# Two-layer mixture-of-experts kernel: both waves' lists cleared by whole stores, first list rows in buffers of their own, list tables and first mixing product moved at the border

## The chip, the cores and the metric

One core of a Trainium2 chip. The metric is the time of one execution on the device in microseconds, the median of three runs. The engines are TensorE (PE), VectorE (DVE), ScalarE (ACT), GpSimd (POOL) and SyncE (SP, which here only issues DMAs).

## The reference

x is 64 samples x 64 channels x 1024 positions in float32. Two layers, each with a residual:

```
x = x + L0_ffn(L0_cond(x, cond_128, ...))
x = x + L1_ffn(L1_cond(x, cond_128, ...))
L0_cond: grouped 1-d convolution (4 groups, 9 taps) + cond @ c_weight.T + bias
L0_ffn:  y @ base_w.T + base_b + 0.5 * sum over the top 2 of 16 experts of w_e * (y @ A.T) @ B_e.T
L1_cond: a 2-layer MLP gives 8 attention weights per sample; out = (sum_k att_k W_k) x + att @ bias_k
L1_ffn:  y @ base_W.T + sum over the top 2 of 28 experts of 2 * g_e * (y @ lora_A_e.T) @ lora_B_e.T
```

## The kernel before, in words

**Tiles.** Rows are (sample, channel) pairs; a tile is 128 rows (2 samples) x 1024 columns, so there are 32 tiles. Every float32 product is made of three float32r products: high x high, high x low, low x high (`three`, L1349 to L1353). So each operand is split in two parts: ACT copies the high one (L736), DVE subtracts for the low one.

**Layer 0, `step0` per tile.** PE convolves tile t+2 (`conv`, into banks c0 and c1), turns tile t+1 (`turn_conv`) and multiplies tile t's y with the weights in three column blocks (`over_y`): bank z2 first (256 base columns, 64 columns of A, 16 router columns), then z0, then z1 (384 columns each), 24 matmuls per block. DVE routes from z2 (`routing`, `list0`), adds the residuals (`residual`, L1199), makes the low parts (`x8_low`, `y_low` L979) and computes each row's rank in its expert's list (`rank0`; the operation at L1036 that writes `before` is the one PE's next block z2 waits for). POOL adds the bias to the next x (L651).

**Lists.** The expert products of layer 0 are not done per tile but over lists sorted by expert, in two waves of 16 tiles. `list0` writes the tile's 64 values times both gate weights into `listed` (L1026), `rank0` the places into `place`, and POOL scatters both rows sets by indirect DMA into `hs_dram[w]` (`scatter`, L665). There is one `listed` buffer of 2 x 64 values; before it is written again, all scatters so far must have landed (semaphore `listed_out`). Behind each expert's list up to the end of a tile of 128 the rows have to be zero. For wave 1 the whole of `hs_dram[1]` is cleared by 17 stores of 512 KB from a zeroed `zt[3]` in steps 12 to 15 (`clear_lists`, L436). For wave 0 16 stores of 128 x 64 zeros go behind the ends of the lists once the counts are known, in step 16 (`pad_lists`, L431 and L432).

**Tables.** When a wave's 16 tiles are ranked, PE and DVE make the tables in three rounds: `count_lists` (rows per expert, tiles per expert), `first_tiles` with DVE's `tiles_of_lists` (prefix sum), `list_tables` (expert and row tile of each of the 48 listed tiles; DVE copies them at L1179 and L1180). `listed_places` (L1187 to L1193) finds every row's place in the results. Then SP reads the tables by register (`value_load`, L442 and L446) and issues four `ht` loads (L443) and four `bd` loads (L449) per listed step (`start_lists`, `listed_step`); PE turns them (`turn_ht`, L1405) and multiplies (`listed_pair`). Wave 0's listed steps run beside tiles 18 to 29, wave 1's beside layer 1's tiles 2 to 13.

**Layer 1, `step1` per tile.** POOL gathers and adds each row's two results from `zs_dram` onto x1 (L677, L685). DVE and ACT build the sample's mixing matrix (`mix`: L1121 to L1130), PE multiplies it with x1 (`mixing`), turns the result (`turn_mixed`, L1474) and runs it over the weights in z2 (252 columns), z0 and z1 (512 each) and over the lora product (`over_h`). The transposes of `hx` (L1601) wait for DVE's routing (`spread1`).

**The border.** Tile 31 of layer 0 and tile 0 of layer 1 overlap. The weights of layer 1 lie where those of layer 0 lay, so each block is split once layer 0's last products on it are done (`w1_high` on ACT, `w1_low` on DVE, L1071; the profile names them `w_0l` and `w_1l`). `mixing(0)` stands between block z0 and block z1 of tile 31. The order on every engine is the order of the program; only semaphores tie engines together.

**SP's order in a step of layer 0:** load `x8raw` of tile t+2 (L407; it waits for the convolution before it), store x1 of tile t-1 (L419), then lists or pads, then load x of tile t+3 (L401; it waits for POOL's residual).

## Time and profile before

| | |
|---|---|
| median of three runs | 1268.43 us (1264.81 to 1268.62) |
| profiled execution, its own time | 1271.76 us |
| its span | 1269.6 us |
| mean granted clock of PE | 0.993 |
| busy: PE, DVE, ACT, POOL | 97%, 50%, 30%, 22% |
| DMA | 258.59 MB, 204 GB/s in the mean |

The time of the profiled execution includes some 2 us around the span. "PE waits" are idle times of PE before an instruction, with what ended them; "DMA to landing" is the time from the issue to the last byte. Names such as `x8raw<-in_x_dram` are output<-input; "PEclk" or "granted clock" is the share of TensorE's 2.4 GHz that it was given.

### The profile page before, as it was taken

How to read it: one execution, taken by the hardware profiler on the slowest of the kernel's cores; microseconds unless marked ns; L12 is line 12 of the kernel's file. 1: busy time of each engine (PE TensorE's matmuls, PEld its weight loads, DVE VectorE, ACT ScalarE, POOL GpSimd, SP SyncE). 2: the span in 40 equal slices, each digit the busy share in tenths (PEclk: the TensorE clock that was granted, in tenths of full speed). 3: DMA queues.
4: the chain of work that ended last, by engine and by line, in shares of the span. 5: the costliest groups of instructions: out<-in, count | busy, mean ns of one | idle time of the engine just before them, and what ended most of it. 6: DMA issues, size and time to landing. Idle time of an engine off the chain costs nothing.

```text
span 1269.6 us, 22120 instructions
## 1 busy us (share of the span) xinstructions
PE 1237.0 (97%) x7264; PEld 1095.3 (86%) x7264; DVE 633.1 (50%) x1809; ACT 376.5 (30%) x801; POOL 279.9 (22%) x309
## 2 busy tenths in 40 slices
PE   6999999999899999998989999999999999999998
PEld 6999999999899999997778787887888888888887
DVE  6666666576444445455645334243344354354452
ACT  4312222121243343324233333334412222222221
POOL 2222222332222222243311121112121211211200
PEclk9999999999899999998999999999999999999999
DMA  7346666665989999967699999999865455455410
GB/s 281 122 141 197 204 192 236 243 233 156 285 272 307 292 306 317 296 226 215 119 227 288 269 269 281 243 299 291 251 145 116 88 120 111 96 118 107 103 50 33
DMA packets 85040, 258.59 MB, mean 204 GB/s; under 512 B 25489, under 2 KB 29969, under 8 KB 77714
## 3 DMA queue, kind: packets, MB, share of 16 engines
q1 hardware_dynamic: 72464, 221.73, 54.3%
q0 software_dynamic: 11264, 35.66, 16.2%
q10 hardware_dynamic: 1266, 0.70, 0.2%
q8 instruction: 15, 0.25, 0.1%
q14 instruction: 31, 0.25, 0.1%
HBM read 154.24 MB, written 103.81 MB: 203 GB/s over the span
## 4 chain that ended last, share of the span: by engine, by line
PE 50%; DVE 2%; DMA 2%; issue 1%; SPq 0%; ACT 0%; POOL 0%; ACTq 0%; POOLq 0%
PE z L1351 14%; PE z L1353 14%; PE z L1352 14%; PE t L1474 2%; PE c L1351 1%; DMA xin<-zs_dram,gpos 1%; PE c L1353 1%; PE c L1352 1%; PE c L1416 1%; PE c L1418 1%; PE prep L1601 1%; PE c L1420 1%; DMA ht<-hs_dram 0%; DVE w_1l L1071 0%; PE t L1420 0%
## 5 line engine op out<-in xcount | busy, mean ns | idle before, releaser
L1351 PE MATMUL z<-w_1h,yh 128*128 128x512 f32 (+1 forms) x504 | 189.0, 375 | 0.0
L1351 PE MATMUL z<-w_0h,yh 128*128 128x512 f32 (+1 forms) x504 | 187.4, 372 | 0.0
L979 DVE TENSOR_TENSOR yl<-t,yh 128x512 fp32r<-128x512 f32 x126 | 81.1, 685 | 211.6 <-ACT yh L736 211.6
L1353 PE MATMUL z<-w_0l,yh 128*128 128x512 f32 (+1 forms) x504 | 184.7, 366 | 0.0
L1353 PE MATMUL z<-w_1l,yh 128*128 128x512 f32 (+1 forms) x504 | 184.7, 366 | 0.0
L1352 PE MATMUL z<-w_0h,yl 128*128 128x512 f32 (+1 forms) x504 | 184.6, 366 | 0.0
L1352 PE MATMUL z<-w_1h,yl 128*128 128x512 f32 (+1 forms) x504 | 184.4, 366 | 0.0
L659 POOL TENSOR_TENSOR carrier<-ones_col 128x1 f32<-128x1 f32 x96 | 23.1, 240 | 672.7 <-DVE den L1045 220.1
L1351 PE MATMUL z<-w_2h,yh 128*128 128x252 f32 (+1 forms) x504 | 151.4, 300 | 5.2 <-DVE before L1036 3.3
L1352 PE MATMUL z<-w_2h,yl 128*128 128x252 f32 (+1 forms) x504 | 150.8, 299 | 0.0
L1353 PE MATMUL z<-w_2l,yh 128*128 128x252 f32 (+1 forms) x504 | 150.6, 299 | 0.0
L736 ACT ACTIVATE yh<-t 128x512 fp32r<-128x512 f32 x126 | 68.4, 595 | 192.2 <-PE t L1392 110.0
L651 POOL TENSOR_TENSOR xb<-xin,bias0b 128x1024 f32<-128x1024 f32 x32 | 81.1, 2534 | 197.2 <-DMA x_dram<-xb 177.1
L1351 PEld LDWEIGHTS z<-w_0h,yh 128*128 128x128 f32 x504 | 94.7, 188 | 19.0 <-issue 8.8
L1351 PEld LDWEIGHTS z<-w_1h,yh 128*128 128x128 f32 x504 | 94.8, 188 | 14.5 <-issue 4.4
L1353 PEld LDWEIGHTS z<-w_1l,yh 128*128 128x128 f32 x504 | 94.7, 188 | 11.6
L1353 PEld LDWEIGHTS z<-w_0l,yh 128*128 128x128 f32 x504 | 94.7, 188 | 11.5
L1352 PEld LDWEIGHTS z<-w_0h,yl 128*128 128x128 f32 x504 | 94.8, 188 | 10.3
L1352 PEld LDWEIGHTS z<-w_1h,yl 128*128 128x128 f32 x504 | 94.8, 188 | 10.1
L1351 PEld LDWEIGHTS z<-w_2h,yh 128*128 128x128 f32 x504 | 95.7, 190 | 7.0 <-DVE before L1036 3.5
L1352 PEld LDWEIGHTS z<-w_2h,yl 128*128 128x128 f32 x504 | 95.8, 190 | 1.4
L1353 PEld LDWEIGHTS z<-w_2l,yh 128*128 128x128 f32 x504 | 95.6, 190 | 0.0
(239 smaller groups left out, 2427.4 us busy)
## 6 DMA issues: line engine op xcount, KB each, us to landing
bd<-bd_dram SPq DMA_DIRECT2D x96, 512.0 KB, 7.7
zs_dram<-zt SPq DMA_DIRECT2D x96, 512.0 KB, 8.7
x8raw<-in_x_dram SPq DMA_DIRECT2D x32, 516.0 KB, 6.4
xin<-in_x_dram SPq DMA_DIRECT2D x32, 512.0 KB, 4.3
x_dram<-xb SPq DMA_DIRECT2D x32, 512.0 KB, 6.9
out_dram<-xb SPq DMA_DIRECT2D x32, 512.0 KB, 2.9
hs_dram<-zt SPq DMA_DIRECT2D x17, 512.0 KB, 6.3
bd_dram<-bd SPq DMA_DIRECT2D x8, 1024.0 KB, 4.8
```

Of the source, the lines that this page charges most:

```text
L651: nc.gpsimd.tensor_tensor(xb[u][:, :], xin[u][:, :], bias0b[:, :], ALU.add).then_inc(xb_ready, 1)
L659: nc.gpsimd.tensor_tensor(carrier[:, :], ones_col[:, :], ones_col[:, :], ALU.add).then_inc(carried, 1)
L736: return nc.scalar.activation(o, i_, ACT.Copy)
L979: V.tensor_tensor(o, v, y_places(s, high, b)[0], ALU.subtract).then_inc(s.y_lo[b], 1)
L1351: T.matmul(o, ah, wh, start=start, stop=False, **kw)
L1352: T.matmul(o, al, wh, start=False, stop=False, **kw)
L1353: return T.matmul(o, ah, wl, start=False, stop=stop, **kw)
L1416: T.matmul(o[half][:, :], hh[ranks(v), j, :], bd[j][ranks(v), 0, w], start=True, stop=False)
L1418: T.matmul(o[half][:, :], hl[ranks(v), j, :], bd[j][ranks(v), 0, w], start=False, stop=False)
L1420: mm = T.matmul(o[half][:, :], hh[ranks(v), j, :], bd[j][ranks(v), 1, w], start=False, stop=True)
L1474: mm = T.transpose(tp[b][:, P * k:P * (k + 1)], mid[:, P * (4 * b + k):P * (4 * b + k + 1)], ident[:, :])
L1601: mm = T.transpose(prepp[0:K1, P * k:P * (k + 1)], hx1[:, K1 * k:K1 * (k + 1)], ident[:, :])
```

## The change

1. **Clearing (SP).** `pad_lists` is gone, with the row counts that it needed (one matmul on PE, two operations on DVE). `clear_lists` now clears both waves: wave 0's 17 stores go in steps 1 to 5, as 4, 4, 3, 3, 3, behind the step's other DMAs.
2. **List rows (POOL, DVE).** There are `HELD = 8` buffers of `listed` and `place`. Tiles 0 to 7 have one each; later ones take buffer t mod 2. `listed_out` is a pair of semaphores by parity: a later tile waits for the scatter of the tile two before it. POOL runs the residuals of tiles 2 to 7, then waits until wave 0 is cleared, then scatters tiles 0 to 5, then goes on as before.
3. **Tables, wave 0 (PE).** `count_lists(0)` stands behind block z2 of tile 16 instead of before it.
4. **Border (PE, DVE, ACT).** `mixing(0)` stands behind the first 12 matmuls of block z1. `rank` and 6 matmuls come before `turn_mixed(0)`. ACT splits three of the four pieces of the first weights before x1 and the routing's exponentials, x1 and the mixing matrix of tile 1 before the next weights. On DVE `mix` is cut in two (`mix_sum`, `mix_low`), the routing of tile 0 of layer 1 comes before `w1_low(1)`.
5. **Tables, wave 1.** `first_tiles(1)` is at the end of tile 0 of layer 1, `list_tables(1)` behind block z2 of tile 1 (before: both in tile 1, the second behind block z0).

```diff
+HELD = 8
-        listed = sb(ctx, "listed", [P, 2, R0])
-        place = sb(ctx, "place", [P, 2], I32)
+        listed = [sb(ctx, f"listed{n}", [P, 2, R0]) for n in range(HELD)]
+        place = [sb(ctx, f"place_of{n}", [P, 2], I32) for n in range(HELD)]
...
+        listed_out = [sem(f"listed_out{u}") for u in range(2)]
...
-            def pad_lists():
-
-                sp.wait_ge(zeros_ready, 5)
-                sp.wait_ge(pad_ready, 1)
-                for e in range(E0):
-                    at = sp.value_load(pad_row[0:1, e, :], min_val=0, max_val=E0 * CAP - P)
-                    sp.dma_start(hs_dram[0][bass.ds(at, P), :], zeros[:, :]).then_inc(pad_out, 16)
-
-            def clear_lists(first, end):
+            def clear_lists(w, first, end):
                 for j in range(first, end):
-                    sp.dma_start(hs_parts[j], zt[3][:, :]).then_inc(cleared, 16)
+                    sp.dma_start(hs_parts[w][j], zt[3][:, :]).then_inc(cleared, 16)
...
             step0(0, 1)
+            clear_lists(0, 0, 4)
             step0(1, 0)
+            clear_lists(0, 4, 8)
             step0(1, 1)
+            clear_lists(0, 8, 11)
...
+            for u in range(2):
+                step0(2, u)
+                split_step(4 + u, u)
+                clear_lists(0, 11 + 3 * u, 14 + 3 * u)
...
-            step0(i, 0, pads=True)
+            step0(i, 0)
...
+            for i in range(1, HELD // 2):
+                for u in range(2):
+                    residual(i, u)
+            pool.wait_ge(cleared, 16 * parts)
+            for t in range(HELD - 2):
+                scatter(t, t % 2, 0, t)
...
-                if not first:
-                    dve.wait_ge(listed_out, 32 * t)
+                if not own_buffers(t):
+                    dve.wait_ge(listed_out[u], 32 * i)
...
-                if at(t, TILES - 1):
-                    mixing(0)
...
+                        mixing(0)
+                        rank(t, w)
+                        over_y(1, w0h, w0l, chunks=range(KC // 2, KC - 2), y=y_of(a0, t))
                         turn_mixed(0)
-                    rank(t, w)
-                    over_y(1, w0h, w0l, stop=True, chunks=range(KC // 2, KC), y=y_of(a0, t)).then_inc(base_done[1], 1)
+                    over_y(1, w0h, w0l, stop=True, chunks=range(KC - 2, KC), y=y_of(a0, t)).then_inc(base_done[1], 1)
...
             exps(a0, TILES - 1)
+            act.wait_ge(base_done[2], TILES)
+            w1_high(0, w1_pieces(0)[0:3])
             act.wait_ge(a0.c_ps[1], TILES)
             x1_high(0, 0, 0)
-            act.wait_ge(base_done[2], TILES)
-            w1_high(0, w1_pieces(0))
+            w1_high(0, w1_pieces(0)[3:4])
...
                 if at(t, 0):
+                    dve.wait_ge(a1.c_out[1], 1)
+                    mix_sum(1)
+                    spread1(0)
+                    x1_low(1, 1)
+                    mix_low(1)
                     w1_low(1, 0, KC // 2)
-                    spread1(0)
...
                 pe.wait_ge(a1.hT_lo, t + 1)
+                if first:
+                    first_tiles(1)
```

The first place is DVE's order in tile 31, the last of layer 0. `listed` is the tile's list rows, `x1l` the low part of layer 1's first tile, `xb` a residual, `w_0l` the low part of layer 1's first weights (two pieces). Before:

```order
L1022 TENSOR_TENSOR before<-before,onehot 128x16 [waits l0_route]
L1026 TENSOR_TENSOR listed<-z,w 128x128 [waits listed_out]
L1116 TENSOR_TENSOR x1l<-xin,x1h 128x1024 [waits x1_hi]
L1199 TENSOR_TENSOR xb<-z,xb 128x256 [waits base_done2]
L1199 TENSOR_TENSOR xb<-z,xb 128x384 [waits base_done0]
L1071 TENSOR_TENSOR w_0l<-w_0raw,w_0h 128x1024 [waits w1_hi0] x2
L1034 TENSOR_TENSOR comb<-z,onehot 128x32 [waits l0_route,rank_ps]
```

Now:

```order
L1031 TENSOR_TENSOR before<-before,onehot 128x16 [waits l0_route]
L1035 TENSOR_TENSOR listed<-z,w 128x128 [waits listed_out1]
L1210 TENSOR_TENSOR xb<-z,xb 128x256 [waits base_done2,xb_ready]
L1080 TENSOR_TENSOR w_0l<-w_0raw,w_0h 128x1024 [waits w1_hi0] x2
L1125 TENSOR_TENSOR x1l<-xin,x1h 128x1024 [waits x1_hi]
L1210 TENSOR_TENSOR xb<-z,xb 128x384 [waits base_done0]
L1043 TENSOR_TENSOR comb<-z,onehot 128x32 [waits l0_route,rank_ps]
```

The wait of `listed` is now on the semaphore of the odd tiles, and one residual and two pieces of weights stand ahead of `x1l`.

The second place is SP's queue in steps 16 and 17. The last four rows of the first piece are the first of 16 pads, each of them these four rows. Before:

```order
L407 DMA x8raw<-in_x_dram 128x1032 [waits l0_c_ps1]
L419 DMA x_dram<-xb 128x1024 [waits l0_z_out2,l0_z_out1,l0_z_out0]
L431 TENSOR_LOAD pad_row [waits pad_ready,zeros_ready]
L431 ISA x2
L432 ISA
L432 DMA hs_dram<-zeros 128x64
```

Now:

```order
L413 DMA x8raw<-in_x_dram 128x1032 [waits l0_c_ps1]
L425 DMA x_dram<-xb 128x1024 [waits l0_z_out2,l0_z_out1,l0_z_out0]
L407 DMA xin<-in_x_dram 128x1024 [waits xb_ready]
L413 DMA x8raw<-in_x_dram 128x1032 [waits l0_c_ps1,bd_out]
L425 DMA x_dram<-xb 128x1024 [waits l0_z_out2,l0_z_out1,l0_z_out0]
L440 TENSOR_LOAD tab_row [waits cleared,tab_ready,listed_out1,listed_out0]
```

The loads of x and `x8raw` and the reads of the table follow the step's store directly.

The third place is SP's queue in steps 1 and 2, where the change has put the first stores:

```order
L425 DMA x_dram<-xb 128x1024 [waits l0_z_out2,l0_z_out1,l0_z_out0]
L407 DMA xin<-in_x_dram 128x1024 [waits xb_ready]
L434 DMA hs_dram<-zt 128x1024 x4
L413 DMA x8raw<-in_x_dram 128x1032 [waits l0_c_ps1]
L425 DMA x_dram<-xb 128x1024 [waits l0_z_out2,l0_z_out1,l0_z_out0]
```

Four stores of 512 KB stand between the load of x and the next load of `x8raw`, which followed each other before.

## Rows read from the trace of the kernel before

**Rows 1.** The page, busy time of the engines: busy us (share), instructions.

```profile
PE 1237.0 (97%) x7264; PEld 1095.3 (86%) x7264; DVE 633.1 (50%) x1809; ACT 376.5 (30%) x801; POOL 279.9 (22%) x309
```

**Rows 2.** PE's waits in the whole span: us in total, times, longest us.

```profile
PE c L1351 <- issue: 6.1, 1, 6.1
PE prep L1405 <- DMA ht<-hs_dram: 5.8, 2, 3.6
PE z L1351 <- DVE before L1036: 3.3, 1, 3.3
...
PE prep L1601 <- DVE hx L1051: 1.4, 1, 1.4
...
PE c L1351 <- DVE mixl L1130: 0.8, 1, 0.8
...
PE prep L1427 <- DVE den L1045: 0.5, 1, 0.5
```

**Rows 3.** Windows: from:to, length, busy us of the five engines, granted clock, DMA share, GB/s.

```profile
217.00:282.00 65.00, 64.54 (x433) 64.13 (x432) 39.26 (x121) 13.20 (x30) 21.88 (x17) 1.00 0.65 237
321.00:327.00 6.00, 6.00 (x22) 6.00 (x23) 2.02 (x8) 0.00 (x0) 2.14 (x3) 0.52 0.99 266
587.30:593.00 5.70, 5.66 (x16) 5.11 (x17) 3.01 (x4) 1.38 (x2) 0.00 (x0) 0.50 1.08 322
640.60:645.00 4.40, 4.39 (x14) 3.55 (x15) 1.12 (x2) 1.33 (x2) 0.00 (x0) 0.61 1.03 225
```

**Rows 4.** SP's queue, timeline 283 to 312: start us, us, line.

```profile
283.34 1.19 SPq L407 DMA_DIRECT2D x8raw<-in_x_dram  x1
...
288.15 17.50 SPq L432 DMA_DIRECT2D hs_dram<-zeros  x16
...
306.22 0.37 SPq L407 DMA_DIRECT2D x8raw<-in_x_dram  x1
...
307.96 4.65 SPq L443 DMA_DIRECT2D ht<-hs_dram  x4
```

**Rows 5.** ACT and DVE timelines, 311 to 318: start us, us, engine, line, [idle before].

```profile
311.77 1.06 ACT L736 ACTIVATE x8h<-x8raw 128x1032 fp32r<-128x1032 f32 x1 [7.59 <-DMA x8raw<-in_x_dram]
...
314.01 2.87 DVE L1187 TENSOR_TENSOR match<-chosen,iota 128x512 f32<-128x512 f32 x1
316.92 0.69 DVE L1189 TENSOR_TENSOR match<-match,first_row 128x512 f32<-128x512 f32 x1
```

**Rows 6.** PE, ACT and DVE timelines at the border, 576 to 591.

```profile
576.87 0.34 PE L1351 MATMUL z<-w_0h,bd 128*128 128x384 f32 x1
...
587.34 0.77 PE L1351 MATMUL c<-x1h,mixh 128*128 128x512 f32 x1 [6.15 <-issue]
...
581.12 1.06 ACT L736 ACTIVATE x1h<-xin 128x1024 fp32r<-128x1024 f32 x1 [2.88 <-DMA xin<-zs_dram,gpos]
...
585.82 0.29 DVE L1026 TENSOR_TENSOR listed<-z,w 128x128 f32<-128x128 f32 x1 [6.26 <-DMA hs_dram<-listed,place]
586.03 1.22 DVE L1116 TENSOR_TENSOR x1l<-xin,x1h 128x1024 fp32r<-128x1024 f32 x1
...
587.96 2.35 DVE L1071 TENSOR_TENSOR w_0l<-w_0raw,w_0h 128x1024 fp32r<-128x1024 f32 x2
```

**Rows 7.** DVE and PE timelines, start of the second wave's lists.

```profile
629.46 0.18 DVE L1180 CAST tab_row<-t 1x48 int32<-1x48 f32 x1
...
640.61 0.51 PE L1405 MATMUL prep<-ident,ht 128*128 128x128 f32 x2 [3.64 <-DMA ht<-hs_dram]
```

**Rows 8.** SP and ACT timelines, 84 to 104; DMA issues; landing times of line L407.

```profile
90.46 0.36 SPq L407 DMA_DIRECT2D x8raw<-in_x_dram  x1
...
102.77 1.09 ACT L736 ACTIVATE yh<-t 128x512 fp32r<-128x512 f32 x2 [5.69 <-PE t L1392]
...
hs_dram<-zt SPq DMA_DIRECT2D x17, 512.0 KB, 6.3
...
DMA to landing us min/median/max: 3.3/6.4/11.1
```

More of the change, by code:

```diff
@@ L348, in build @@
         x1_t = x1_dram.rearrange("(t p) l -> t p l", p=P)
-        hs_parts = hs_dram[1].rearrange("(p j r) c -> j p (r c)", p=P, c=R0, r=L // R0)
+        hs_parts = [a.rearrange("(p j r) c -> j p (r c)", p=P, c=R0, r=L // R0) for a in hs_dram]
+        parts = hs_parts[0].shape[0]
         b0_pair = b0_in_order.rearrange("(p s) r l -> p (s r) l", s=2)
@@ L489, in _, with step0 @@
             load_x(0, 1)
-            def step0(i, u, first=False, lists=None, more=True, pads=False, start=False):
+            def step0(i, u, first=False, lists=None, more=True, start=False):
                 t = 2 * i + u
@@ L699, in _ @@
             residual(0, 1, first=True)
+            for i in range(1, HELD // 2):
+                for u in range(2):
+                    residual(i, u)
+            pool.wait_ge(cleared, 16 * parts)
+            for t in range(HELD - 2):
+                scatter(t, t % 2, 0, t)
+            i = HELD // 2
             for u in range(2):
-                scatter(u, 0, u)
-                residual(1, u)
-            with pool.Fori(2, NA // 2 + 1) as i:
+                scatter(HELD - 2 + u, u, 0, HELD - 2 + u)
+                residual(i, u)
+            with pool.Fori(HELD // 2 + 1, NA // 2 + 1) as i:
                 for u in range(2):
                     t = 2 * i + u - 2
-                    scatter(t, 0, t)
+                    scatter(t, u, 0, t)
                     residual(i, u)
-            pool.wait_ge(cleared, 16 * hs_parts.shape[0])
+            pool.wait_ge(cleared, 16 * WAVES * parts)
             with pool.Fori(NA // 2 + 1, TILES // 2) as i:
@@ L1249, in _ @@
             list_numbers()
-            with dve.Fori(2, 6) as i:
+            for t in range(4, HELD):
+                step0(t // 2, t % 2, 0, split=True)
+            with dve.Fori(HELD // 2, 6) as i:
                 for u in range(2):
@@ L1326, in step1 @@
                         .then_inc(a1.z_out[b], 1)
-            step1(0, 0, first=True, count=True)
-            step1(0, 1, first=True, tiles=True, turn=WS)
+            step1(0, 0, first=True)
+            step1(0, 1, first=True, tables=True, turn=WS)
             step1(0, 2, places=True, turn=WS + 1)
@@ L1573, in _, with step1 @@
                 step0(t, 1)
-            def step1(t, first=False, last=False, tiles=False, lists=False, turn=None):
+            def step1(t, first=False, last=False, tables=False, lists=False, turn=None):
                 s = t - S1_LISTS + WS
@@ L1586, in step1 @@
                     count_lists(1)
-                if tiles:
-                    first_tiles(1)
+                if tables:
+                    list_tables(1)
                 if lists:
@@ L1598, in step1 @@
                     listed_pair(s, 1)
+                if tables:
+                    pe.wait_ge(tab_ready, 4)
                 pe.wait_ge(a1.hx, 2 * t + 2)
@@ L1631, in _ @@
             step1(0, first=True)
-            step1(1, tiles=True, turn=WS)
+            step1(1, tables=True, turn=WS)
             with pe.Fori(S1_LISTS, S1_LISTS + WS - 1) as t:
```

151 lines of the change are left out of this document (71 added, 80 removed).

## The prediction

> **What bounds the kernel now.** I read the page first: TensorE (PE) is busy 1237.0 of the span's 1269.6 us [rows 1], so nothing that another engine does faster counts unless it closes a hole of PE. The next view is PE's list of waits [rows 2]. The reader is to see that the holes are few and single: a matmul of the first mixing product waits once for 6.1 us, the transposes of `ht` twice for 5.8 us together (once for 3.6, so once for 2.2), the first projection of a tile once for 3.3 us on `before`, and 1.4, 0.8 and 0.5 us are single waits too. The steady steps have none. The third view is the table of windows [rows 3]: in an ordinary stretch the granted clock is 1.00, but behind each of the three large holes stands a stretch of 4 to 6 us where PE is busy all the time at a clock of about 0.5, that is at 1.2 instead of 2.4 GHz. A hole is paid twice: its length, and then the work behind it at half speed.
>
> The price of the second part is length times the missing clock: 6.0 x 0.48 = 2.9 us behind the first wave's start, 5.7 x 0.50 = 2.9 us at the border, 4.4 x 0.39 = 1.7 us at the second wave's start [rows 3].
>
> So there are three places: step 16 to 18 (first wave's lists start), the border between the layers, and the second tile of the second layer (second wave's lists start).
>
> **Part A, start of the first wave.** The change removes the 16 stores of zeros behind the lists. They hold SP's queue for 17.50 us, from 288.15 [rows 4]. Behind them stand the load of the next `x8raw` (at 306.22) and the four `ht` loads (from 307.96, 4.65 us) [rows 4]. Both waits of PE come from this. The `x8raw` load is late, ScalarE (ACT) sits idle 7.59 us for it, VectorE (DVE) makes the low part only then, and `listed_places` and the tile's last steps, `before` among them, slide behind [rows 5]; that is the 3.3 us. The `ht` loads land late; that is the 2.2 us. With the queue free, the `x8raw` load can go when the convolution before it is done, some 7 us earlier, and the `ht` loads as much earlier, more than three times their hole. The 0.5 us wait on `place` goes because the count of the lists now stands behind 24 matmuls. Removed: 0.5 + 2.2 + 3.3 + 2.9 = 8.9 us. What is late next is `listed_places`, which has to fit between the residuals of the tile and its last y. Its first operation took 2.87 us where the next one, of the same size, took 0.69 [rows 5], and a residual of GpSimd ran beside it. If GpSimd's residual meets it again, DVE is done about 1.2 us after PE wants it; if not, 0.8 us before (0.69 for 2.87 makes up 2.2). The row lies nearer to a partial meeting, so I leave 0.5 us. Net 8.4, between 7.7 and 8.9.
>
> The Trainium skill (SBUF — State Buffer, Who interferes with whom) says of the port pair that DVE and GpSimd share that the one that issues second "fully blocks" until the first is done. By that rule it would be 1.2 us if GpSimd goes first and nothing otherwise. The pair of rows 5 agrees with a block of one operation.
>
> **Part B, the border.** DVE stood 6.26 us before `listed` of the last tile, until 585.82, because both `listed` buffers' scatters shared one semaphore and the last but one had to land; the low part of x1 came behind it at 586.03, and the mixing product at 587.34 [rows 6]. Now each parity has its own semaphore, and tile 31 waits for tile 29's rows, which went out a step earlier. The next limit is x1, the gathered tile itself: ACT starts its high part only at 581.12, when the gather lands, and takes 1.06 us [rows 6]. PE reaches this place at 587.34 - 6.15 = 581.2. The change puts 12 matmuls of bank 1 ahead of the mixing product; 24 such took 4.3 us (576.87 to 581.2) [rows 6], so 12 take 2.15 and PE asks for x1's low part at 583.35. DVE now does two pieces of `w_0l` first (2.35 us [rows 6]), which end at about 582.5, then x1's low part (1.22 [rows 6]): 583.7. A hole of about 0.4 us is left.
>
> Behind the mixing product (six matmuls of 512 columns, at full clock 1.4 us by 4.3/24 x 512/384 each) PE has rank, 12 matmuls and 8 transposes, some 3.2 us, to 588.4. DVE, after the mixing product's end at 585.2, has to do the seven small rank operations (estimated at 1.1 us), two more pieces of `w_0l` (2.35 us [rows 6]) and then y's first half (0.6 us, half of `x1l`'s width): about 589.4. So a new hole of about 1 us; I count 1.1. Further on, the routing of the first tile of layer 1 now comes before the low parts of the third weights, so the 1.4 us before the transposes of `hx` go; the 0.8 us before the second mixing product go too, since the sum and both low parts are moved ahead of the 4.6 us of weights. Removed 6.1 + 1.4 + 0.8 + 2.9 = 11.2, given back 0.4 + 1.1 = 1.5. Net 9.7; ends 8 (both new holes twice as large) and 11.2.
>
> **Part C, start of the second wave.** Before, the table was ready at 629.46 and PE could turn `ht` at 640.61, after 3.64 us of idling [rows 7]: 11.15 us from table to use, all of it SP's reads of the table, its issues and the landing. The change moves the prefix sum to the end of the tile before and the tables right behind the next tile's first 24 matmuls. By the order of the work on DVE that is about 7 us earlier against PE's own step. 7 against a hole of 3.64 leaves 3.4 us of slack. Removed 3.6 + 1.7 = 5.3. The tables now stand ahead of that tile's mixing and routing, as the tile sums did before: I give back 0.3. Net 5.0, between 0 (the loads land as late as before, because the DMA share in this stretch is 1.03 [rows 3]) and 5.3.
>
> **Part D, what is added.** 17 stores of 512 KB are put on SP's queue in steps 1 to 5 (4, 4, 3, 3, 3), and GpSimd (POOL) holds back all scatters of the first wave until they have landed. Cover for the stores: in steps 12 to 15 the kernel before does just this with the same 17 stores for the other wave, the last five right ahead of an `x8raw` load at 283.34 [rows 4], and PE is busy 64.54 of 65.0 us there, all of the rest being the 0.5 us above [rows 3]. Cover for the scatters: the first eight tiles have buffers of their own; the backlog of six costs POOL some 16 us in steps 6 and 7, when the next residual waits for a store anyway. If both covers hold, nothing. The narrow place is step 4: its `x8raw` load went at 90.46 even before, since SP waits for the attention's round trip, and behind it on ACT stands the y of the next tile, which is due at 102.77 [rows 8]. Three more stores ahead of the round trip, each issued in about 1.1 us, move the load by 3.4 us, to 94. Landings of `x8raw` go from 3.3 to 11.1 us, the median is 6.4 [rows 8]. At the median it is there at 100.3, in time; at 11.1, the landing behind a crowd, at 105, and a tile's y is some 5 us late. The load is nearer to the median, since the stores ahead of it have landed by the end of the round trip; I take 0.5 us for this part and keep the other for the range.
>
> The Trainium skill (DMA: Bandwidth & Descriptors, Queues, rings and completion order) speaks against the change here: on one ring descriptors are consumed in order, so a load waits for whatever was queued ahead of it. By that rule the sum would be some 5 us worse.
>
> **Sum.** 8.4 + 9.7 + 5.0 - 0.5 = 22.6 us. The profiled execution took 1271.8 us (span 1269.6), so it would take 1249.2. The median of the runs, 1268.4, lies 3.3 us below it; the holes are the same in both, so the median goes to 1245.8, said as 1246. A measurement of this kernel can tell about 0.3% (3.8 us) from no change.
>
> **Rivals.**
> - *The `ht` loads of the second wave stay late.* The DMA engines, not the table, set the landing. For it: share 1.03 behind that hole [rows 3]. Against: the loads are 32 KB each and start 7 us earlier. Price: part C goes, 5.0 us, so 1251.
> - *The stores bite in step 4 or 5.* With the landing of 11.1 us x8raw is there at 105 instead of 100.3 [rows 8]; ACT's y, due at 102.77, comes up to 5 us late, and the half clock behind it costs 2.9 as in rows 3. The page of the Trainium skill named in part D would have it so. Once: 1246 + 8 = 1254; twice: 1262. Against: rows 3 and 4 of steps 12 to 15.
> - *Slower than before.* The same mechanism in every one of the five steps with stores, as POOL's residual waits for the store of x1 and SP's next load for the residual, so that lateness is handed on. At 5 + 2.9 us each it is 39 us: 1285. It decides from 5.3 us per step on, where five of them eat the 22.6 and 3.8. Against it: a step is 16 us long, and 12 to 15 hand nothing on.
> - *The border's wait only changes its name.* x1's gather, at 581.12, lands later than before since nothing holds it: a microsecond of lateness is a microsecond on PE. Above 3 us of it the half clock comes back as well: 1246 + 3 + 2.9 = 1252.
>
> **How the numbers follow.** Forecast 0.66 (1243 to 1249), late `ht` 0.10, border 0.08, step 4 or 5 0.12, slower 0.04. The lower bound is all removed and nothing given back: 8.9 + 11.2 + 5.3 = 25.4, so 1243; a microsecond less for the scatter of three runs: 1242. The upper end takes in the late `ht`, the border and one bite: 1254. Faster 0.95, same 0.01, slower 0.04.
>
> **What would show it.** In the new profile PE's waits should have no entry above 1.5 us but the first load's; `before` and `ht` are gone from the list; all windows between 40 us and the end show a clock of 1.00; busy PE stays near 1230 us (the half-clock stretches counted as busy); ACT's wait for `x8raw` in steps 2 to 6 is below 3 us. It would be wrong if PE waits in the first 130 us, if the mixing product still waits over 3 us, or if a clock of 0.5 stands behind any of the three places.

## The result, and the profile after

| | before | after |
|---|---|---|
| median of five runs | 1268.62 us (1264.81 to 1271.12) | 1256.15 us (1253.37 to 1258.99) |
| profiled execution, its own time | 1271.76 | 1253.69 |
| its span | 1269.6 | 1251.9 |

The ratio is 0.9902, 95% interval 0.9874 to 0.9929: faster, by 12.5 us. The prediction was 1246 (1242 to 1254): the direction is right, the gain is about half of the 22.6 us forecast, and the median lies above the range.

The page of after, busy time of the engines, answers to [rows 1]:

```profile
PE 1228.3 (98%) x7263; PEld 1093.2 (87%) x7263; DVE 636.9 (51%) x1807; ACT 376.2 (30%) x801; POOL 286.7 (23%) x307
```

PE's waits in the whole span of after answer to [rows 2] (us in total, times, longest us):

```profile
PE z L1367 <- DVE before L1045: 5.0, 4, 2.0
PE z L1367 <- DVE yl L987: 2.9, 2, 1.9
PE c L1367 <- DVE x8l L969: 1.3, 3, 0.7
...
PE z L1503 <- issue: 0.8, 1, 0.8
PE z L1367 <- DVE rank L1047: 0.7, 1, 0.7
PE c L1368 <- issue: 0.6, 1, 0.6
```

The 6.1 us of the mixing product, the 5.8 of `ht` and the 3.3 of `before` are gone. But `before` has come back with four waits, up to 2.0 us. PE's timeline says where (start us, us, [idle before]):

```profile
124.23 0.45 PE L1367 MATMUL z<-w_2h,yh 128*128 128x336 f32 x1 [2.04 <-DVE before L1045]
143.03 0.41 PE L1367 MATMUL z<-w_2h,yh 128*128 128x336 f32 x1 [1.07 <-DVE before L1045]
157.03 0.18 PE L1503 MATMUL z<-onehot,small_upper 128*128 128x32 bf16 x1 [0.81 <-issue]
...
163.77 0.41 PE L1367 MATMUL z<-w_2h,yh 128*128 128x336 f32 x1 [0.71 <-DVE rank L1047]
181.65 0.42 PE L1367 MATMUL z<-w_2h,yh 128*128 128x336 f32 x1 [1.69 <-DVE before L1045]
```

These rows all stand between 120 and 185 us, in steps 5 to 8 (the fourth wait for `before` is one of 0.17 us at 277.85; of the two for `yl` the 1.9 us one is at 20.28, in the first tile). The windows of after show in their columns PE's busy time and the granted clock (length first, clock behind POOL's busy time):

```profile
289.00:303.00 14.00, 14.00 (x96) 13.43 (x95) 10.28 (x35) 1.79 (x7) 3.87 (x4) 1.00 0.82 300
303.00:324.00 21.00, 21.00 (x143) 20.67 (x142) 14.79 (x42) 3.84 (x9) 8.07 (x5) 1.00 0.49 134
576.00:594.00 18.00, 16.63 (x102) 15.56 (x101) 12.98 (x41) 7.90 (x13) 8.94 (x10) 1.00 0.96 266
613.00:634.00 21.00, 20.60 (x113) 17.10 (x113) 10.07 (x30) 4.97 (x11) 6.35 (x8) 1.00 0.92 204
121.00:137.00 16.00, 13.96 (x78) 13.76 (x77) 8.46 (x30) 2.33 (x6) 0.41 (x2) 0.89 0.80 296
137.00:153.00 16.00, 14.93 (x101) 14.68 (x100) 10.31 (x29) 4.15 (x9) 13.88 (x15) 1.00 0.62 213
153.00:169.00 16.00, 13.63 (x81) 12.83 (x80) 7.57 (x22) 1.77 (x6) 10.85 (x12) 0.89 0.35 111
```

The first four are the three places of [rows 3]: PE runs at clock 1.00 in all of them. The last three are the new place, twice at 0.89. Length times the missing clock is 1.8 us each time. The half clock is seen behind the hole of 2.04 us: from 124.20 to 128.00 the granted clock is 0.55, from 143.00 to 147.00, behind the hole of 1.07 us, it is 1.00.

Holes alone don't give the balance. For that I took from both PE timelines the start of block z2 of every tile (in before 320.98 for tile 18, in after 327.37, and so on) and subtracted stretch by stretch:

| stretch (start of z2) | before | after | difference | predicted |
|---|---|---|---|---|
| up to tile 4 | 90.12 | 89.62 | -0.5 | 0 |
| tile 4 to 10 | 95.55 | 108.07 | **+12.5** | +0.5 |
| 10 to 16 | 96.31 | 96.20 | -0.1 | 0 |
| 16 to 19, part A | 61.44 | 53.17 | -8.3 | -8.4 |
| 19 to 30 | 216.71 | 216.77 | +0.1 | 0 |
| 30 to tile 1 of layer 1, part B | 58.73 | 49.46 | -9.3 | -9.7 |
| tile 1 to 3 of layer 1, part C | 49.33 | 43.26 | -6.1 | -5.0 |
| tile 3 to 31 of layer 1 | 580.40 | 574.61 | **-5.8** | 0 |
| the rest | 21.0 | 20.7 | -0.3 | 0 |

The sum is, but for rounding, the 17.7 us between the spans. Three terms came out within 1.1 us. Two stretches that the prediction had at about nothing moved by 12.5 and 5.8 us, in opposite directions, and in the bare total the second hides half of the first.

### The profile page after: what moved, and what is told of

Read it like the earlier page. It is cut to its first block, busy times and chain, and to the rows that moved or that the text cites. A ratio compares the mean times of both kernels' runs of the same rounds, so it can differ in the third digit from the quotient of the medians.

```text
span 1251.9 us, 21917 instructions
## 1 busy us (share of the span) xinstructions
PE 1228.3 (98%) x7263; PEld 1093.2 (87%) x7263; DVE 636.9 (51%) x1807; ACT 376.2 (30%) x801; POOL 286.7 (23%) x307
## 4 chain that ended last, share of the span: by engine, by line
PE 85%; DMA 5%; DVE 3%; issue 2%; POOL 2%; SPq 2%; ACT 1%; ACTq 0%; POOLq 0%; DVEq 0%
PE z L1367 22%; PE z L1369 21%; PE z L1368 21%; DMA x8raw<-in_x_dram 3%; PE c L1367 3%; PE c L1369 3%; PE c L1368 3%; PE c L1432 2%; PE t L1488 2%; PE c L1434 2%; PE c L1436 2%; PE t L1408 2%; DMA x_dram<-xb 1%; SPq L434 1%; POOL hs_dram L665 1%
## 5 line engine op out<-in xcount | busy, mean ns | idle before, releaser
L650 POOL TENSOR_TENSOR xb<-xin,bias0b 128x1024 f32<-128x1024 f32 x32 | 86.2, 2695 | 265.7 <-DMA x_dram<-xb 246.8
L1367 PEld LDWEIGHTS z<-w_0h,yh 128*128 128x128 f32 x504 | 94.6, 188 | 17.8 <-issue 8.7
L1369 PEld LDWEIGHTS z<-w_1l,yh 128*128 128x128 f32 x504 | 94.6, 188 | 10.6
L1210 DVE TENSOR_TENSOR xb<-z,xb 128x384 f32<-128x384 f32 (+1 forms) x96 | 48.3, 508 | 104.2 <-PE z L1369 95.7
```

Source lines behind the costliest of these rows:

```text
L650: nc.gpsimd.tensor_tensor(xb[u][:, :], xin[u][:, :], bias0b[:, :], ALU.add).then_inc(xb_ready, 1)
L1210: V.tensor_tensor(o, z[b][:, 0:w.stop - w.start], o, ALU.add).then_inc(a0.z_out[b], 1)
L1367: T.matmul(o, ah, wh, start=start, stop=False, **kw)
L1369: return T.matmul(o, ah, wl, start=False, stop=stop, **kw)
```

## The experiments

There are twelve runs. "Tile 4 to 10" is the measure of the early stretch; "layer-1 step" is the start of z2 of layer 1's last tile less that of tile 15, divided by 16, which no hole touches. The three p-kernels and after_again ran on one chip (before: 1266.57 us there), g_spread, h_behind, lay448 and instr1 on a second (before: 1268.83), f_behind, border_pe and the two shifts on a third (before: 1267.93). Between chips the ratios to before are the fairer comparison, and the stretches of the traces the sharper one.

| run | tile 4 to 10 | tile 16 to 19 | layer-1 step | time us (runs) |
|---|---|---|---|---|
| before | 95.55 | 61.44 | 19.27 | see above |
| after | 108.07 | 53.17 | 19.06 | 1256.15 (5) |
| after_again | 111.77 | 53.17 | 19.05 | 1259.66 (5) |
| p_none | 95.96 | 62.24 | 19.28 | 1258.69 (5) |
| p_hold | 103.22 | 60.79 | 19.28 | 1262.24 (10) |
| p_stores | 103.78 | 60.06 | 19.28 | 1266.00 (10) |
| g_spread | 102.42 | 53.17 | 19.05 | 1249.37 (6) |
| h_behind | 95.80 | 53.17 | 19.05 | 1243.03 (4) |
| f_behind | 101.80 | 53.25 | 19.06 | 1250.74 (4) |
| border_pe | 95.80 | 53.17 | 19.06 | 1247.18 (4) |
| lay448 | 111.56 | 53.35 | 19.28 | 1266.5 (1) |
| instr1 | 109.00 | 53.22 | 19.05 | 1257.95 (1) |
| shift64 | 95.64 | 53.09 | 19.11 | 1241.7 (1) |
| shift256 | 96.28 | 53.18 | 19.05 | 1244.04 (1) |

### Which half of part D: the stores or the held scatters

Four kernels on one chip. All three p-kernels have the pads back, so that the first wave's lists need no clearing:

```diff
 # p_none: no wave-0 stores, scatters as before; pads back (SP, PE, DVE as in before)
-            clear_lists(0, 0, 4)
...
-            for i in range(1, HELD // 2):
-                for u in range(2):
-                    residual(i, u)
-            pool.wait_ge(cleared, 16 * parts)
...
+            for i in range(1, HELD // 2 + 1):
+                for u in range(2):
+                    scatter(2 * i + u - 2, u, 0, 2 * i + u - 2)
+                    residual(i, u)
 # p_hold: p_none, but POOL's order as in the change, without the wait on cleared
 # p_stores: p_none, but the 17 stores of steps 1 to 5, into spare_dram
```

> The change with its whole-store clearing of the first wave taken out: no stores of zeros in steps 1 to 5, GpSimd's scatters between its residuals as before the change, and the 16 pads back at the first wave's start. The buffers of the lists' first rows, the border and the second wave's tables stay as changed. What is computed is complete. Measure: start of PE's block z2 of tile 10 (before 185.67, after 197.69) for the early steps, tile 19 less tile 17 for the wave's start. Both theories, that SP's 17 stores cost the early 12.6 us (S) and that GpSimd's held scatters do (P), expect tile 10 at 185.2 to 185.7. The wave's start costs its 8.4 us again (PE waits for ht and x8l near step 17), the border and the second wave's start keep 9.3 and 5.9: time 1268.6 - 15.2 = 1253.4 (1251 to 1256). A third theory, that the buffers or the parity semaphores of the listing cost the early time (B), expects tile 10 at 190 or later.

> As p_none, but GpSimd makes residuals 2 to 7 first and then scatters 0 to 5 in one run, as in the change (without a wait for the stores, which are not there). Theory P (the backlog of scatters is the early loss): residual 8 starts at 155 or later (before 144.76), tile 10 starts at 190 or later, time 5 us or more above p_none. Theory S (SP's stores are): residuals 2 to 7 start every 15.9 us as before, the last at 129; the backlog then runs from 131 to about 152, so residual 8 is a few us late (148 to 153) once, and tile 10 starts at 185.2 to 188; time 0 to 3 us above p_none.

> As p_none, but SP issues the 17 stores of zeros of steps 1 to 5 (4, 4, 3, 3, 3), into a tensor of their own that nothing reads; GpSimd's scatters stay between its residuals. Theory S: ACT waits 3 to 6 us for x8raw in steps 3 to 6, GpSimd's residual comes 3 us and more late in each step with stores, meets DVE's b_low (3.4 us instead of 1.2), and PE waits from step 5 on; tile 8 starts at 158 to 164 (before 153.82), tile 10 at 190 to 198, time 5 to 12 us above p_none. Theory P: the waits of ACT are there but PE has none over 1 us, tile 10 at 185.2 to 187, time within 1.5 us of p_none.

> The changed kernel as it is, on the same chip as the three. The early loss is of the change and not of one execution: tile 10 starts at 196 to 199 again, GpSimd's residual 8 at 158 or later. Its steps in layer 1 show whether the 19.06 us a step of the one profile of after (19.27 before) is the change's or an execution's: if the change's, tile 30 of layer 1 less tile 3 takes 27 steps of 19.06 again and the time is 1251 to 1254; if an execution's, it lies anywhere from 19.0 to 19.3 and the time at 1253 to 1259. DVE's and ACT's waits of 5 and 9 us behind signals of PE in step 7 come again if they belong to GpSimd's backlog.

Measured against before's 1266.57 on that chip: p_none 1258.69 (ratio 0.9936, 0.9910 to 0.9963), p_hold 1262.24 (0.9964, 0.9946 to 0.9982), p_stores 1266.00 (0.9979, 0.9956 to 1.0003), after_again 1259.66 (0.9936, 0.9911 to 0.9961).

p_none has no early loss (95.96), so the buffers and the parity semaphores are innocent. p_stores loses 7.8 us there, p_hold 7.3, and both by times too (7.3 and 3.6 us above p_none). In p_hold's time only half of the 7.3 shows; its profile was 1.2 us quicker than p_none's up to tile 4 and 1.5 quicker at the pads. Tile 10 starts at 193.97 in p_stores, where theory S had put it, and at 193.17 in p_hold, where theory P had put it. Each of the two theories had bet that the other half costs little; neither is right alone. The two halves add up to 15.1, and the change has both: 12.1 us over p_none in the profile of after, 15.8 in after_again. So the loss is real and differs by some 4 us between executions. With that after_again missed its own expectation: tile 10 at 204.10 instead of 196 to 199, and 1259.66 us instead of 1251 to 1254, though its steps of layer 1 took 19.05 us again. p_hold went against its expectation in a second way: residual 8 was 7 us late, as foreseen, but this isn't what PE waits for. That is taken up below.

p_none came out at 1258.7 and not at the 1253.4 expected, though B (49.56) and C (43.55) are there. Between the profiles of before and p_none the spans differ by 12.7 us: 9.2 and 5.8 from B and C, less 1.0 up to tile 4, 0.4 up to tile 10 and 0.8 at the pads. The times differ by 7.9 only, as before's profiled execution (1271.8) took longer than the median of its runs on this chip (1266.6).

### The loop that the stores close

PE waits for `before` of DVE, and DVE is late since ACT is. ACT's timeline in after:

```profile
97.80 1.07 ACT L743 ACTIVATE x8h<-x8raw 128x1032 fp32r<-128x1032 f32 x1 [3.10 <-DMA x8raw<-in_x_dram]
...
116.58 1.07 ACT L743 ACTIVATE x8h<-x8raw 128x1032 fp32r<-128x1032 f32 x1 [5.91 <-DMA x8raw<-in_x_dram]
...
135.35 1.07 ACT L743 ACTIVATE x8h<-x8raw 128x1032 fp32r<-128x1032 f32 x1 [4.42 <-DMA x8raw<-in_x_dram]
```

The distances are 18.8 us, where a step of PE is 15.93. Something with a period of its own runs here. The chain of waits of after, 98 to 120 us (start us, us, what), is that loop:

```profile
98.90 1.23 DVE x8l L969
100.14 3.34 DVE bd L1074
...
103.49 0.34 SPq L420
...
103.88 0.43 SPq L416
...
104.36 1.10 SPq L434
...
105.50 1.57 SPq L434
...
107.11 1.89 SPq L434
...
109.04 7.52 DMA x8raw<-in_x_dram
116.58 1.08 ACT x8h L743
...
117.68 1.23 DVE x8l L969
118.92 3.33 DVE bd L1074
```

DVE makes the low part of `bd`; SP waits for it and stores it (L420), loads the next `braw` (L416), issues three stores of zeros (L434, 4.6 us in all), and only then the load of `x8raw`, which lands behind them after 7.5 us; ACT and DVE split it, and DVE's next `bd` stands behind that in DVE's order. The link "SP waits for `bd`" exists in steps 4 to 11 only (`split_step`). In steps 12 to 15, which the prediction took as cover, the same 17 stores close no loop. Nor do they in steps 1 to 3 of after, which have 4, 4 and 3 stores and no wait for `bd`: up to tile 4 nothing is lost (89.62 against 90.12), and ACT has no wait for `x8raw` there. A kernel with the wait for `bd` alone taken out was not run.

The second contribution is in the `bd` row itself. DVE and POOL timelines of after:

```profile
118.83 3.40 DVE L1074 TENSOR_TENSOR bd<-braw,bd 128x1024 fp32r<-128x1024 f32 x1
...
157.24 1.21 DVE L1074 TENSOR_TENSOR bd<-braw,bd 128x1024 fp32r<-128x1024 f32 x1
```

```profile
117.94 3.21 POOL L650 TENSOR_TENSOR xb<-xin,bias0b 128x1024 f32<-128x1024 f32 x1 [15.56 <-DMA x_dram<-xb]
...
160.59 2.39 POOL L650 TENSOR_TENSOR xb<-xin,bias0b 128x1024 f32<-128x1024 f32 x1
```

The lateness shifts POOL's residual onto DVE's `bd`: together they take 3.4 and 3.2 us where each alone takes 1.2 and 2.4. In before and in h_behind the two do not meet in steps 4 to 11. The meeting makes up 2.2 of the 18.8 us; without it the loop would take an estimated 16.6, still more than PE's step. The store of x1 that frees the residual's buffer comes from the same queue. The Trainium skill (SBUF — State Buffer, Who interferes with whom) says that the one that issues second "fully blocks". The trace agrees for DVE, whose operation ends 1.1 us after POOL's (122.23 and 121.15). It doesn't for POOL, which had started first and took 0.8 us longer all the same.

If this loop is the cause, the stores may stay where they are in number, and only have to leave the piece of queue between `bd`'s store and `x8raw`'s load. Two kernels ask that, with POOL's backlog spread in both:

```diff
 # g_spread: 6, 6, 5 stores at the end of steps 1, 2, 3, none in 4 and 5
-            clear_lists(0, 0, 4)
+            clear_lists(0, 0, 6)
...
 # h_behind: 4, 4, 3, 3, 3 as in the change, but in step0, behind store_x1
             def step0(...):
                 if exists(t + 2):
                     load_x8(t + 2)
                 if not first:
                     store_x1(i + u - 1, 1 - u)
+                if clears is not None:
+                    clear_lists(*clears)
 # POOL in h_behind (g_spread: the wait behind residual 5, then scatters
 # 0 1 2, 3 4, 5 6 and 7 ahead of residuals 6, 7, 8 and 9)
+            for t in range(2, 7):
+                residual(t // 2, t % 2)
+            pool.wait_ge(cleared, 16 * parts)
+            for held_back, t in (((0, 1, 2), 7), ((3, 4, 5, 6), 8), ((7,), 9)):
+                for n in held_back:
+                    scatter(n, n % 2, 0, n)
+                residual(t // 2, t % 2)
```

> The changed kernel with both causes of the early loss taken away: the first wave's 17 stores go into steps 1 to 3 alone (6, 6, 5; steps 1 to 3 lost nothing in any run so far), and GpSimd makes residuals 2 to 5, waits for the stores, and then works its scatters off two or three at a time between residuals 6 to 9 (0 1 2, 3 4, 5 6, 7) instead of seven in one run. Theory T (stores 7.3 in steps 4 to 7 and the run of scatters 6.1 in step 7 add up to the early loss): tile 10's z2 starts at 185.5 to 188 (after 197.7 and 204.1, p_none 187.1), no hole over 2 us before tile 16; time 1259.7 - 13.4 = 1246 (1243 to 1249). Rival (any 17 stores ahead of tile 8 delay the stores of x1 and the loads behind them): the loss moves to steps 2 to 4 and stays at 5 us and more: 1251 and more.

> The changed kernel with its 4, 4, 3, 3, 3 stores kept in steps 1 to 5 but issued directly behind the store of x1, ahead of SP's wait for the residual and the load of the next tile, instead of at the step's end behind bd's stores; GpSimd's scatters spread (0 1 2, 3 to 6, 7). If the place on SP's queue is what makes the x1 store and x8raw late (each found stores of the step before still ahead of it), the stores now drain while SP waits: loss in steps 4 to 7 at most 2 us instead of 7.3, tile 10 at 186 to 189, time 1247 (1244 to 1250). If it is the amount in steps 4 and 5 that counts (loads of braw, stores of bd and of x1 fill the queues there), the loss stays 4 to 8 us: tile 10 at 190 to 195, 1250 to 1254.

h_behind has no early loss at all (95.80 against 95.96 of p_none). It takes 1243.03 us, ratio to before 0.9789 (0.9751 to 0.9826), and is faster than both kernels: 13.1 us below the change by the medians, 14 by the ratios. Its ACT timeline has no wait for `x8raw` over 0.9 us in steps 2 to 7:

```profile
113.93 1.07 ACT L738 ACTIVATE x8h<-x8raw 128x1032 fp32r<-128x1032 f32 x1 [0.90 <-DMA x8raw<-in_x_dram]
130.07 1.05 ACT L738 ACTIVATE x8h<-x8raw 128x1032 fp32r<-128x1032 f32 x1
```

g_spread was a miss: 1249.37 (0.9838, 0.9806 to 0.9869). It has neither the loop nor the run of scatters, and loses 6.5 us, nearly all in step 4. That is the rival written down with it, a loss that moves to steps 2 to 4 and stays at 5 us and more; only its time, 1251 and more, was put too high. SP's and ACT's timelines show it:

```profile
89.13 4.89 SPq L434 DMA_DIRECT2D hs_dram<-zt  x5
94.06 2.40 SPq L416 DMA_DIRECT2D braw<-in_b_dram  x2
96.50 0.64 SPq L524 DMA_DIRECT2D att_dram<-att  x1
101.85 1.13 SPq L527 DMA_DIRECT2D attb<-att_dram  x2
103.03 0.58 SPq L413 DMA_DIRECT2D x8raw<-in_x_dram  x1
```

```profile
107.86 1.06 ACT L739 ACTIVATE x8h<-x8raw 128x1032 fp32r<-128x1032 f32 x1 [9.48 <-DMA x8raw<-in_x_dram]
```

This is the prediction's own "narrow place": SP can't go on before the attention's round trip is back, and the five stores ahead of it push it to 101.85; the `x8raw` load goes at 103.03 instead of 90.46 [rows 8]. In h_behind it goes at 92.18. p_stores and h_behind have the same stores in the same steps, and lose 7.8 us and nothing: the place on the queue decides.

### A run of scatters delays TensorE's signals

In p_hold and in after, DVE and ACT wait for PE without any reason in the profile. PE's timeline in f_behind, which has h_behind's stores and the change's POOL order, so the scatters of tiles 0 to 6 in one run:

```diff
 # f_behind: h_behind, with
-            for t in range(2, 7): ... (spread, as above)
+            for i in range(1, HELD // 2):
+                for u in range(2):
+                    residual(i, u)
+            pool.wait_ge(cleared, 16 * parts)
+            for t in range(HELD - 2):
+                scatter(t, t % 2, 0, t)
```

> As h_behind (stores directly behind the store of x1), but GpSimd's work as in the change: residuals 2 to 7, then scatters 0 to 5 in one run, then 6, residual 8, 7, residual 9. If the run of scatters by itself delays PE's signals (p_hold lost 6.1 us so in step 7): tile 8's z2 starts at 161 to 163 (h_behind 155.85), PE shows gaps of about 1 us put down to issue while GpSimd issues, time 1243 + 6 = 1249 (1247 to 1251). If p_hold's hole was one execution's accident or came from residual 8 alone: tile 8 at 156 to 158, time 1243 to 1245.

```profile
150.28 0.34 PE L1365 MATMUL z<-w_1h,yh 128*128 128x384 f32 x1 [0.59 <-issue]
...
152.42 0.34 PE L1367 MATMUL z<-w_1l,yh 128*128 128x384 f32 x1 [1.09 <-issue]
...
153.82 0.46 PE L1365 MATMUL z<-w_1h,yh 128*128 128x384 f32 x1 [1.06 <-issue]
```

DVE's timeline of the same kernel:

```profile
148.88 0.17 DVE L994 COPY lg<-z 128x16 f32<-128x16 f32 x1 [7.93 <-remote]
...
154.72 0.56 DVE L1208 TENSOR_TENSOR xb<-z,xb 128x384 f32<-128x384 f32 x1 [2.79 <-remote]
```

The windows of f_behind, length and PE's busy time first, the granted clock behind POOL's:

```profile
145.00:151.00 6.00, 4.76 (x27) 4.33 (x25) 1.56 (x11) 1.64 (x6) 4.86 (x8) 1.00 0.11 36
151.00:157.00 6.00, 3.60 (x11) 3.11 (x11) 3.21 (x9) 0.94 (x1) 3.91 (x3) 0.74 0.13 36
```

The early loss is 6.0 us over h_behind (tile 8's z2 at 161.62 against 155.85), the time 1250.74 (0.9867, 0.9831 to 0.9902), 7.7 above, on another chip. PE idles for 3.6 of the 6.0 us in these two windows, and the missing clock of the second is 1.6 more. The gaps begin ahead of residual 8, which starts at 152.85, so it is not their cause. So the run of scatters costs 6.0 and 7.3 us of the early stretch by itself, with the stores of f_behind and without any in p_hold (7.7 and 3.6 by the times); p_hold shows the same gaps at 148.64 to 153.60. By what mechanism is not shown. DVE reads the logits of block z2 (`lg`) 3.9 us after the block starts in p_none (143.03 less 139.13), but 9.2 after it here (148.88 less 139.65): PE's signal comes 5.3 us late. Then single matmuls start with gaps of up to 1.1 us, at the pace of POOL's indirect DMAs. Here is that pace, from POOL's timeline of p_hold:

```profile
143.08 0.96 POOL L679 DMA_INDIRECT hs_dram<-listed,place_of  x1 [0.30 <-issue]
...
144.42 0.98 POOL L679 DMA_INDIRECT hs_dram<-listed,place_of  x1 [0.16 <-issue]
```

In p_hold it ran from 131 to 152 without a break. In h_behind there is a run of three tiles (119 to 128) and one of four (133 to 145). Behind the first the signal of z2 is 1.2 us late (128.99 less 123.92 is 5.1, against 3.9), behind the second 2.1 us (145.84 less 139.89 is 6.0), but PE has no hole of either. So the lateness grows with the run, and what a step of these kernels can bear lies between 12 and some 20 us in a row.

### The 5.8 us that nobody had predicted

Layer 1's steps are 1.1% shorter in after and after_again than before, though every step there is PE without a hole at clock 1.00, with the same instructions. They are as long as before in all three p-kernels. Against after these have more instructions on PE (the pads' matmul) and more SBUF: the buffer of zeros and three rows, 448 bytes per partition ahead of the weights.

```diff
 # lay448: after, with
+        unused = sb(ctx, "unused", [P, R0 + 3 * E0])
         tile_no = sb(ctx, "tile_no", [E0, LISTED])
 # shift64, shift256: h_behind, with [P, 16] and [P, 64] there
 # instr1: after, with the pads' matmul in count_lists(0), which nothing reads
```

> The changed kernel with 448 bytes of SBUF per partition allocated and not used, where the buffer of zeros and the pads' three rows lay: every tile behind them, the weights included, lies where it lies in p_none. Steps of layer 1: 19.06 us in after and after_again, 19.28 in p_none, p_hold, p_stores, 19.27 before. If the place of the weights in SBUF sets that rate: 19.28 a step (22.5 in all lost over layer 1's steps against after: about 6 us), time 6 us above after. If the program (the matmul of the pads, instructions moved by it) does: 19.06.

> The changed kernel with one matmul more on TensorE, the one that the pads had in count_lists(0), with no reader: TensorE's instructions behind it lie as in p_none, SBUF as in after. If the position of instructions sets the rate of layer 1's steps: 19.28 us a step. If the place of the tiles in SBUF does: 19.06.

> h_behind with 64 bytes of SBUF per partition unused ahead of the weights. 448 bytes there cost 0.22 us per step of layer 1 (19.06 to 19.28). If the step's time depends on the place modulo 128 bytes or less, 64 bytes more (448 is 64 modulo 128) give 19.28 as well; if on a coarser one, 19.06 or another value. Layer 0's steps 9 to 15 (15.98 us) may change too. Time 1243 or 1249 accordingly.

> h_behind with 256 bytes of SBUF per partition unused ahead of the weights. If the step's time depends on the place modulo 128 or 256 bytes: 19.06 us per step of layer 1 and the time of h_behind, 1243. If it depends on a coarser place or on a neighbour (which tiles share a region with the weights): 19.2 to 19.3 or another value, up to 1249.

instr1 keeps 19.05, lay448 has 19.28: it is the place in SBUF of the tiles behind those 448 bytes. These two and the two shifts are single executions, but the step repeats within 0.01 us in all kernels with the same layout. Groups of PE by form, 960 to 1200 us (count, then busy us and mean ns of one), first of after, then of lay448:

```profile
L1368 PE MATMUL z<-w_0h,yl 128*128 128x512 f32 x102 | 39.8, 390 | 0.0
```

```profile
L1369 PE MATMUL z<-w_0h,yl 128*128 128x512 f32 x101 | 39.9, 395 | 0.0
```

The same matmul takes 5 ns less. From start to start, in the mean of the same stretch, the matmuls of block z0 are 227.7 ns apart in after and 233.2 in lay448, those of z1 232.9 and 236.7; with 24 in each block that is the 0.22 us. The mixing product, as wide, has 232.8 and 233.6, the narrower block z2 116.7 and 116.5. So the matmuls on `w_0` and `w_1` change and the others hardly do; which of the moved tiles is the cause was not tried. shift64 gives 19.11, shift256 again 19.05, as without a shift; 448 is 192 modulo 256. The four values fit a dependence on the place modulo 256 bytes, which is not shown beyond them. Layer 0 answers in its own way: tiles 10 to 15 take 15.93 us each before and in shift64, 15.97 in h_behind. Over the tiles 4 to 31 of layer 1 the difference of after and lay448 is 6.2 us. It is no merit of the change's design; it came with the 448 bytes of the pads that the change no longer needs.

### What of the border is PE's move

```diff
 # border_pe: h_behind, with mixing(0) back ahead of z1's first 12 matmuls
+                if at(t, TILES - 1):
+                    mixing(0)
                 if not first:
                     pe.wait_ge(a0.z_out[1], t)
```

> h_behind with one thing of the border undone: TensorE's mixing product for the first tile of layer 1 is back ahead of bank z1's first 12 matmuls in tile 31; ScalarE's and VectorE's orders and the semaphores by parity stay as changed. If the scatter's semaphore was most of the old hole, x1's low part is ready at about the same time against the step as in h_behind, some 2.3 us after PE now asks for it: a hole of 2.5 to 3 us in place of 0.4, perhaps with half clock behind it: 1243 + 2.2 to 5 = 1245 to 1248. If the move on TensorE was most of it: a hole of 5 us and more, half clock behind it, 1251 and more.

The hole ahead of the mixing product is 2.4 us (0.5 in h_behind), tile 30 to tile 1 of layer 1 takes 52.97 us instead of 49.50, and the time is 1247.18 (0.9835, 0.9800 to 0.9870), 4.2 above h_behind's on another chip; the intervals of the two ratios overlap, so the trace is the better witness. A part is half clock again: from 576 to 594 us the granted clock is 0.91, in h_behind 1.00. So of the border's 9.3 us some 3.5 come from the move of the mixing product on TensorE, and the rest from DVE no longer waiting for a scatter and from the other orders, which were not tried apart.

## Why the prediction was right and wrong

**Part A, right.** 8.3 us against 8.4. In after, `x8raw` is loaded 0.2 us after tile 17's z2 starts (311.47 and 311.23), before 7.1 us after it (306.22 and 299.12), the "some 7 us" of the prediction, and the `match` rows that took 2.87 and 0.69 us [rows 5] do not meet a residual:

```profile
321.91 0.68 DVE L1198 TENSOR_TENSOR match<-chosen,iota 128x512 f32<-128x512 f32 x1
322.63 0.69 DVE L1200 TENSOR_TENSOR match<-match,first_row 128x512 f32<-128x512 f32 x1
```

p_none, with the pads back, takes 62.24 us for tile 16 to 19, h_behind 53.17: the pads are worth 9.1. One sum in the term was off: 1.2 us less the 2.2 is 1.0 before PE wants it, not 0.8. It changes nothing, as `listed_places` held nobody up.

**Part B, right, and by its steps.** 9.3 against 9.7. In after no wait stands before `listed` of the last tile, at 583.26. The prediction puts this down to the semaphores alone and speaks of two `listed` buffers; before the change there was one, so the second buffer is as much part of it. The two holes that I had left at 0.4 and 1.1 us are there at 0.37 and 0.99, in the PE timeline of after, which answers to [rows 6]:

```profile
587.38 0.47 PE L1367 MATMUL c<-x1h,mixh 128*128 128x512 f32 x1 [0.37 <-issue]
...
593.14 0.35 PE L1367 MATMUL z<-w_2h,yh 128*128 128x252 f32 x1 [0.99 <-DVE yl L987]
```

**Part C, right, a little small.** 6.1, of which 0.4 is the shorter step of layer 1, against 5.0. The table is ready at 616.76, 3.5 us behind the start of tile 1's z2 (613.29), where it had been 10.6 behind it (629.46 and 618.86): the "about 7 us earlier" of the prediction. PE turns `ht` at 630.74 without idling; the 11.15 us between table and use [rows 7] have become 14.0. The 0.3 that I gave back was not needed.

**Part D, wrong: this is the step that failed.** It said 0.5 us, and it was 12.5 (12.1 over p_none, 15.8 in a second execution). Both covers failed, each in its own way. For the stores the cover was "in steps 12 to 15 the kernel before does just this". It does so in steps whose SP queue has no wait for `bd`. With that wait in the step the stores lie on a closed chain of DVE, SP, the load and ACT, which came to 18.8 us against PE's 15.93. I had put down `x8raw`'s launch in step 4 (94, measured 92.9), and its landing as a single event. That load landed in 4.9 us, at 97.78, well before the 100.3 that I took to be in time. But I had held it against ACT's y at 102.77 and not against the operation that reads it: in before ACT made `x8h` at 95.08. And I never went once around from one `bd` to the next: the next `x8raw` load went at 109.04, before at 106.37. For the scatters the cover was that the backlog "costs POOL some 16 us, when the next residual waits for a store anyway". That counts POOL's time alone; what it cost was PE's and DVE's, 6 to 7 us through late signals, which no row of before could show, since before has no such run.

The Trainium skill's rule on ring order (DMA: Bandwidth & Descriptors, Queues, rings and completion order) had been set aside with the same cover. It was named at some 5 us; the stores cost 7.8, and the load behind three stores landed in 7.5 us instead of the median 6.4 [rows 8]. The rule's direction was right.

**What was missing from the sum.** 5.8 us of gain in layer 1, from the place of the tiles in SBUF. The sum with both: 22.6 - 12.0 (part D) + 5.8 (place) + 1.1 (C) - 0.1 (A) - 0.4 (B) + 0.8 (the other stretches) = 17.8, and the spans are 17.7 apart. The medians lie only 12.5 apart: after's profile was one of its quicker runs (1253.7 of up to 1259.0), before's lay above the highest of the five (1271.8 against 1271.1), and the early stretch of the change varies by 4 us.

**The chances.** "The stores bite in step 4 or 5", at 0.12, was nearest in mechanism and in time (once 1254, twice 1262; measured 1256.2). That the time came so near is partly luck, as the gain of 5.8 us in layer 1 stands against a larger loss, and the half of that loss that the run of scatters makes stands in no rival. The rival should have had most of the chance, and it asked for the right sign of it: ACT's wait for `x8raw` above 3 us in steps 2 to 6, which came at 3.1, 5.9 and 4.4. The slower case, 1285, needed lateness handed on through all five steps. It was handed on, but only from step 4 on, once the loop is closed. The rival on the border's wait had the half clock come back above 3 us of lateness; in after it is there behind a hole of 2.04 us. Of the signs of being wrong the first came true: PE waits in the first 130 us, at 124.23.

## What to carry to other kernels

When work is added to a queue, go once around every chain that passes through it, from a load to the operation that lets the next load of its kind be issued, and compare that sum with the step of the bounding engine; a stretch where the same addition was harmless is cover only if the queue's waits there are the same. Put added stores behind the last urgent load of the step and ahead of the queue's next long wait, where in h_behind they cost nothing. When comparing two kernels, compare the length of steps that the change does not touch as well: here 448 bytes that went moved everything behind them in SBUF and gave 0.5% of the time.

## What was unexpected of the hardware

- A run of indirect DMAs on GpSimd, one each 1.3 us for some 20 us, delays other engines' work: DVE got PE's signal up to 5.3 us late, and single matmuls started with gaps of up to 1.1 us in the middle of block z1, where the program has no wait. It cost 7.3 us of the early stretch in p_hold and 6.0 in f_behind; the mechanism is open. A run of 12 us in h_behind delayed a signal by 2.1 us and cost nothing.
- The time of a 512-column float32r matmul depended on where the tiles lay in SBUF: 390 ns in the mean, 395 with 448 bytes of shift. The step of layer 1 went from 19.05 to 19.28 us with 448 bytes, to 19.11 with 64, and was 19.05 again with 256.
- A residual on GpSimd and a two-input subtraction on DVE at the same time took 3.2 and 3.4 us, against 2.4 and 1.2 alone: the one that had started first was slowed as well.
